# A displaced, smoothed residual on one core: shorter tile heads, narrower frame copies, and another order of the blocks

## The chip, the cores and the metric

The kernel runs on one core of one Trainium2 chip. The metric is the device time of one execution in microseconds (us), as the median of three runs. PE is the matrix engine (TensorE), DVE the vector engine (VectorE), ACT ScalarE, POOL GpSimd; SP (SyncE) only issues DMAs here, and all loads and stores go through its one queue.

## The reference, cut to what matters

`x` is 16 images of 768 channels of 64 x 64 float32 values, `offset` 48 pairs of displacements. The result is `x + conv(shift(group_norm(x)))`:

```python
# group norm: 32 groups of 24 channels, mean and variance over (24, 64, 64) of one image
n = (x - mean) / sqrt(var + 1e-5)
off_px = offset * 64                        # 48 positions, each for 16 neighbouring channels
off_int = round(off_px); sub = off_px - off_int
dx, dy = off_int[:, 0], off_int[:, 1]       # one pair for each position
shifted[r, c] = n[r - dy, c - dx]           # zero where that lies outside the 64 x 64 image
kern = exp(-((kx + sub_x)**2 + (ky + sub_y)**2) / 0.5), normalised   # 3 x 3, kx and ky in -1, 0, 1
out = x + conv3x3(shifted, kern, padding="SAME")                     # each channel by itself
```

The offsets are a 7 x 7 grid without its centre, from -48 to 48 pixels in steps of 16 in both directions, each moved by a random number of deviation 0.64 pixels. A large displacement leaves only a small window of the image that gets anything added.

## The kernel before, in words

**Tiles.** One tile is one position (16 channels) of 8 images: 128 partitions of 4096 float32 values, 2.1 MB. There are 48 positions and two halves of the images, so 96 tiles, and each is loaded once and stored once in place: SBUF holds ten slots of one tile each (`xs`, `SLOTS`). Three neighbouring positions are a block (48 channels, two groups); a block of one half is a unit, so there are 32 units of three tiles.

**Statistics of a unit.** PE sums the tiles of the next unit over the partitions (L289, 16 instructions a tile). ACT reduces that sum (L463), PE spreads it (L304 to L306), ACT copies it out as means (L470, L476), and squares each tile against its mean (L484, about 3.9 us with its accumulator read). PE spreads the squares (`variances`, L346 to L354), ACT scales them (L492), and POOL makes from them three column weights for each tile (L253, then L257, L260, L266 three times).

**The tile itself.** ACT copies the rows of the tile that the window needs into `frame`, with the mean subtracted (`fill_frame`, L417); `frame` has a border of zeros. DVE then makes five passes over the window, all of them SCALAR_TENSOR_TENSOR: L704 and L709 smooth along the row into `smooth`; L713, L716 and L719 add the smoothed rows to the tile in `xs` with the three column weights. Window heights and widths are rounded up to one of four sizes, `SIDES = [64, 50, 34, 18]`, and each of the 16 combinations is a branch of its own, chosen at run time from a word read into a register (`choose`, L185). For this the loop over tiles (`tile_of`, L751) has a head of register instructions: the loop's own, L727, L732, the branches, and L704's addresses. L708 reads the four words of the next tile.

**What waits for what.** `frame` is single: ACT may fill it for the next tile once L709 of this one is done. L713 needs the column weights of its tile. POOL's weights need the variances, which for the heavier unit of a pair need the first two tiles of the next unit loaded and summed, since PE runs its instructions in the written order.

**Order of the units.** `PAIRS` lists pairs of blocks. A pair (a, b) gives four units: a and b of the first half of the images, a and b of the second. The window sizes (rows x columns) of the three tiles of each block, worked out from the offsets:

| Block | Tiles | Block | Tiles |
|---|---|---|---|
| 0 | 18x18, 18x34, 18x50 | 8 | 64x50, 64x34, 64x18 |
| 1 | 18x64, 18x50, 18x34 | 9 | 50x18, 50x34, 50x50 |
| 2 | 18x18, 34x18, 34x34 | 10 | 50x64, 50x50, 50x34 |
| 3 | 34x50, 34x64, 34x50 | 11 | 50x18, 34x18, 34x34 |
| 4 | 34x34, 34x18, 50x18 | 12 | 34x50, 34x64, 34x50 |
| 5 | 50x34, 50x50, 50x64 | 13 | 34x34, 34x18, 18x18 |
| 6 | 50x64, 50x34, 50x18 | 14 | 18x34, 18x50, 18x64 |
| 7 | 64x18, 64x34, 64x50 | 15 | 18x50, 18x34, 18x18 |

**SP's queue.** Ten loads, then in a fixed order stores and loads: the store of tile n waits until DVE has finished that tile (L202), the load of tile n + 10 until the store of tile n has landed (L197). The queue is in order, so a store whose tile is late holds up the loads behind it. The last load is issued after the store of tile 86, and only stores follow.

**Setup.** DVE works out all table entries in `smooth` (L581 to L669), one instruction after another, each waiting for the one before; then it sums the third tile (L677), which the first unit's means need.

Of the kernel before, what the change touches and what calls it, by code (L numbers as in the profile page):

```python
# [5 lines left out]
def build(nc, x, offset, out):  # L6
    f32 = mybir.dt.float32
    i32 = mybir.dt.int32
# [4 lines left out]
    P = 128  # L13
# [10 lines left out]
    UT = 3  # L24
# [21 lines left out]
    PAIRS = [(9, 4), (3, 13), (5, 0), (7, 2), (10, 14), (8, 1), (6, 11), (12, 15)]  # L46
# [13 lines left out]
    KIND, TO, FROM, COLUMN = range(WORDS)  # L60
    ROW_BITS = (H - SIDES[-1]).bit_length()

    ctx = ExitStack()
    with ctx:
# [19 lines left out]
        small = sb("small", [P, 54])  # L84
# [9 lines left out]
        col_flat = small[:, 27:45]  # L94


        own_mean = small[:, 45:48]
        own_sum = small[:, 48:49]
        mean_64 = small[:, 49:51]
        spread = small[:, 51:53]  # L100

        last_sum = small[:, 53:54]
        col_w = col_flat.rearrange("p (u k) -> p u k", k=3)
        base_w = xs[:, SLOTS * PIX:].rearrange("p (n k) -> p n k", k=3)
        side_w = [sb(f"side_w{k}", [P, TILES]) for k in range(2)]
        words = sb("words", [P, WORDS * (TILES + 1)], i32)
        fills = sb("fills", [P, TILES], i32)
# [15 lines left out]
        word_of = words[:, 0:WORDS * TILES].rearrange("p (n k) -> p n k", k=WORDS)  # L123
# [102 lines left out]
        def _(pool):  # L226
# [13 lines left out]
            for i in range(2 * UT):  # L240
                V.memset(word_of[:, :, COLUMN].rearrange("p (u i) -> p u i", i=2 * UT)[:, :, i], 3 * i)

            V.memset(words[:, WORDS * TILES:], 0).then_inc(slots_ready, 1)
# [6 lines left out]
            def weights(u):  # L250
# [4 lines left out]
                for i in range(UT):  # L255
# [10 lines left out]
                    V.tensor_scalar(col_w[:, now * UT + i, :], base_w[:, position, :], rstd0[:, column],  # L266
# [111 lines left out]
        def _(act):  # L378
# [13 lines left out]
            def load_fill(n):  # L392
                act.reg_load(entry, fills[0:1, bass.ds(n, 1)])  # L393

            def fill_frame(u, i, last=False):


                word = act.snap(entry, min_val=0, max_val=(len(SIDES) << ROW_BITS) - 1)
                row = word & (1 << ROW_BITS) - 1
                rows_kind = act.snap(word >> ROW_BITS)  # L400
# [4 lines left out]
                act.reg_mov(copy_from, base + row * W)  # L405
                act.reg_mov(copy_to, row * PITCH + PAD * PITCH)
# [3 lines left out]
                def emit(k):  # L410
                    rows = SIDES[k]
                    a = act.snap(copy_from, min_val=0, max_val=(SLOTS - 1) * PIX + (H - rows) * W)
                    b = act.snap(copy_to, min_val=PAD * PITCH, max_val=(PAD + H - rows) * PITCH)
                    if not first:

                        act.wait_ge(smooth_ready, act.snap(frames, min_val=1, max_val=TILES))
# [360 lines left out]
```

## Time and profile before

| | us |
|---|---|
| median of 3 runs (973.67 to 978.83) | 973.79 |
| the profiled execution's own time | 979.06 |
| its span | 977.1 |
| DVE busy | 824.8 (84%) |
| PE busy | 785.6 (80%) |
| ACT busy | 638.9 (65%) |
| POOL busy | 368.1 (38%) |
| DMA, share of 16 engines | 98.0% |
| bytes moved | 403.09 MB, mean 413 GB/s |

The profile's page divides the span into 40 slices and gives for each the busy tenths of every engine, and the rate of the DMA engines. A line of the list of groups, or of the list by shape, says which line of the kernel ran on which engine, how often, its busy time and its mean duration; behind it stands how long the engine was idle just before, and what it waited for. Windows give the same busy times for stretches of the span. Every duration in this document is of the one profiled execution, whose time is 979.06 us.

### The profile page before, as it was taken

How to read it: one execution, taken by the hardware profiler on the slowest of the kernel's cores; microseconds unless marked ns; L12 is line 12 of the kernel's file. 1: busy time of each engine (PE TensorE's matmuls, PEld its weight loads, DVE VectorE, ACT ScalarE, POOL GpSimd, SP SyncE). 2: the span in 40 equal slices, each digit the busy share in tenths (PEclk: the TensorE clock that was granted, in tenths of full speed). 3: DMA queues.
4: the chain of work that ended last, by engine and by line, in shares of the span. 5: the costliest groups of instructions: out<-in, count | busy, mean ns of one | idle time of the engine just before them, and what ended most of it. 6: DMA issues, size and time to landing. Idle time of an engine off the chain costs nothing.

```text
span 977.1 us, 9088 instructions
## 1 busy us (share of the span) xinstructions
PE 785.6 (80%) x2132; PEld 383.6 (39%) x2132; DVE 824.8 (84%) x551; ACT 638.9 (65%) x461; POOL 368.1 (38%) x348
## 2 busy tenths in 40 slices
PE   0998987979979698897979879689797997979820
PEld 0544443434434343353434434345343443434410
DVE  7587988777798997978889899898998979797795
ACT  7778676564766747678466746577675785774661
POOL 0214034340432624013254393463845438250312
PEclk9999988989979799897998979989898897989955
DMA  9999999999999999999999999999999999999948
GB/s 364 427 401 423 392 405 429 429 429 428 430 429 430 432 428 414 430 429 430 431 429 406 398 433 376 407 419 393 431 408 430 430 427 431 431 431 430 430 208 343
DMA packets 27821, 403.09 MB, mean 413 GB/s; under 512 B 3216, under 2 KB 3216, under 8 KB 3216
## 3 DMA queue, kind: packets, MB, share of 16 engines
q1 hardware_dynamic: 27792, 402.71, 98.0%
q8 instruction: 17, 0.28, 0.1%
q14 instruction: 12, 0.10, 0.0%
HBM read 201.38 MB, written 201.33 MB: 412 GB/s over the span
## 4 chain that ended last, share of the span: by engine, by line
DVE 28%; DMA 27%; PE 20%; POOL 7%; issue 7%; ACT 5%; DVEq 3%; ACTq 2%; SPq 0%; POOLq 0%
PE sum_ps L289 17%; DMA out_dram<-xs 15%; DMA xs<-x_dram 12%; DVE xs L713 6%; DVE xs L716 6%; DVE smooth L709 6%; DVE smooth L704 6%; DVE xs L719 4%; POOL small L253 2%; POOL small L260 2%; ACT frame L417 2%; POOL small L257 2%; ACT unused L484 2%; POOL small L266 1%; ACTq L393 1%
## 5 line engine op out<-in xcount | busy, mean ns | idle before, releaser
L289 PE MATMUL sum_ps<-xs,bands 128*128 128x512 f32 x976 | 483.5, 653 | 51.2 <-DMA xs<-x_dram 51.2
L484 ACT ACTIVATE unused<-xs,small 128x4096 bf16 (+1 forms) x94 | 348.3, 3706 | 8.3 <-ACT small L470 4.8
L417 ACT ACTIVATE frame<-xs,small (+1 forms) x96 | 223.3, 2326 | 184.3 <-DVE smooth L709 183.3
L289 PEld LDWEIGHTS sum_ps<-xs,bands 128*128 128x128 f32 x976 | 200.6, 210 | 295.4 <-issue 282.2
L253 POOL TENSOR_TENSOR small<-small 128x3 f32<-128x3 f32 x32 | 41.6, 1299 | 570.6 <-ACT small L492 570.6
L289 PE MATMUL sum_ps<-xs,halves 128*128 128x512 f32 x496 | 230.0, 619 | 17.4 <-DMA xs<-x_dram 17.4
L704 DVE SCALAR_TENSOR_TENSOR smooth<-frame,side_w 128x612 f32 (+5 forms) x96 | 163.6, 1705 | 72.2 <-ACT frame L417 37.1
L713 DVE SCALAR_TENSOR_TENSOR xs<-smooth,small,xs 128x612 f32 (+5 forms) x96 | 163.5, 1703 | 51.9 <-POOL small L266 49.6
L709 DVE SCALAR_TENSOR_TENSOR smooth<-frame,side_w,smooth x96 | 159.7, 1664 | 7.5 <-DVE smooth L704 4.1
L719 DVE SCALAR_TENSOR_TENSOR xs<-smooth,small,xs 128x594 f32 (+9 forms) x96 | 159.8, 1664 | 3.4
L716 DVE SCALAR_TENSOR_TENSOR xs<-smooth,small,xs 128x594 f32 (+9 forms) x96 | 159.7, 1664 | 3.4
L289 PEld LDWEIGHTS sum_ps<-xs,halves 128*128 128x128 f32 x496 | 97.4, 199 | 146.4 <-issue 119.3
L266 POOL TENSOR_SCALAR small<-xs,small 128x3 f32<-128x3 f32 x96 | 119.5, 1245 | 9.5
L260 POOL TENSOR_SCALAR small<-small 128x1 f32<-128x1 f32 x96 | 106.6, 1110 | 8.4
L257 POOL TENSOR_SCALAR small<-small 128x1 f32<-128x1 f32 x96 | 99.7, 1039 | 3.3
L463 ACT ACTIVATE sum_ps<-sum_ps 128x512 f32<-128x512 f32 x31 | 18.0, 581 | 73.8 <-PE sum_ps L289 71.0
L304 PE MATMUL mean_ps<-small,halves 128*128 128x1 f32 x62 | 13.0, 279 | 61.6 <-ACT sum_ps L463 61.6
L304 PEld LDWEIGHTS mean_ps<-small,halves 128*128 128x128 f32 x62 | 10.7, 217 | 74.3 <-ACT sum_ps L463 74.3
L470 ACT ACTIVATE small<-mean_ps 128x3 f32<-128x3 f32 x31 | 5.4, 175 | 27.6 <-PE mean_ps L306 27.6
L492 ACT ACTIVATE small<-var_ps,small 128x3 f32<-128x3 f32 x32 | 8.2, 255 | 22.6 <-PE var_ps L354 21.7
L346 PEld LDWEIGHTS var_ps<-small,bands 128*128 128x128 f32 x62 | 11.9, 194 | 18.8 <-issue 18.8
L484 ACT ACTIVATION_READ_ACCUMULATOR unused<-xs,small 128x1 f32 x94 | 17.5, 186 | 0.0
(132 smaller groups left out, 259.3 us busy)
## 6 DMA issues: line engine op xcount, KB each, us to landing
xs<-x_dram SPq DMA_DIRECT2D x96, 2048.0 KB, 14.8
out_dram<-xs SPq DMA_DIRECT2D x96, 2048.0 KB, 17.7
smooth<-offset_dram SPq DMA_DIRECT2D x1, 48.0 KB, 4.1
```

The lines of the kernel that those rows point to most:

```text
L253: V.tensor_tensor(rstd0, var, power, ALU.pow).then_inc(rstd_step, 1)
L257: V.tensor_scalar(fix[:, column], var[:, column], rstd0[:, column], rstd0[:, column], ALU.mult, ALU.mult).then_inc(rstd_step, 1)
L260: V.tensor_scalar(rstd[:, column], fix[:, column], -0.5, 1.5, ALU.mult, ALU.add).then_inc(rstd_step, 1)
L266: V.tensor_scalar(col_w[:, now * UT + i, :], base_w[:, position, :], rstd0[:, column], rstd[:, column], ALU.mult, ALU.mult).then_inc(col_w ...
L289: last = nc.tensor.matmul(sum_ps[:, :], (FIRST, SAME, SECOND)[i], slot_px(n, c * BANK, (c + 1) * BANK), start=(i == 0 and c == 0), stop=(i ...
L417: nc.scalar.activation(frame[:, bass.ds(b, rows * PITCH)].rearrange("p (r c) -> p r c", c=PITCH)[:, :, LEFT:LEFT + W], xs[:, bass.ds(a, ro ...
L484: nc.scalar.activation(unused[:, :], xs[:, bass.ds(n % SLOTS * PIX, PIX)], ACT.Square, bias=neg_mean[:, i:i + 1], accum_out=squares[:, i:i ...
L704: V.scalar_tensor_tensor(sm, frame_window(beside, cols), side_w[0][:, bass.ds(n, 1)], frame_window(src, cols), ALU.mult, ALU.add).wait_op( ...
L709: V.scalar_tensor_tensor(part, frame_window(behind, cols - 1), side_w[1][:, bass.ds(n, 1)], part, ALU.mult, ALU.add).wait_op(half_smooth, ...
L713: V.scalar_tensor_tensor(x_window(0, rows), sm, col_flat[:, bass.ds(weights + 1, 1)], x_window(0, rows), ALU.mult, ALU.add).wait_op(smooth ...
L716: V.scalar_tensor_tensor(x_window(1, rows), sm[:, 0:rows - 1], col_flat[:, bass.ds(weights, 1)], x_window(1, rows), ALU.mult, ALU.add).wai ...
L719: V.scalar_tensor_tensor(x_window(0, rows - 1), sm[:, 1:rows], col_flat[:, bass.ds(weights + 2, 1)], x_window(0, rows - 1), ALU.mult, ALU. ...
```

## The change

It has three parts.

**Heads and words.** The tile loop now counts from 1, so that the loop's register is itself the count that semaphores are compared with. The register instructions of L727 and L732 (copies of the count, the address to the side, the address behind) are gone from the head: the address to the side is now a word of its own (`BESIDE`, in place of `COLUMN`), and the address behind is worked out between the first and the second pass. The column of weights is found by a remainder, `done % (2 * UT)`, in the address of each of the three adding passes. The read of the next tile's words moves from between the first and second pass to between the second and third. The column weights have a buffer of their own with another layout, and the words for ACT lie in the other 64 partitions of `words`.

In the DVE program, the head of the tile loop and the first two passes of one branch (18 x 18) before; `words` is the table of words, `side_w` the weights along the row, ISA a register instruction:

```order
L751 ISA
L727 REGISTER_ALU
L727 ISA
L732 ISA
L185 COMPARE_AND_BRANCH x4
L704 ISA
L704 SCALAR_TENSOR_TENSOR smooth<-frame,side_w 128x324
L708 ISA
L708 TENSOR_LOAD words
L709 ISA
L709 SCALAR_TENSOR_TENSOR smooth<-frame,side_w,smooth 128x18x17
```

And the same place now, up to the third pass:

```order
L773 ISA
L191 COMPARE_AND_BRANCH x4
L730 ISA
L730 SCALAR_TENSOR_TENSOR smooth<-frame,side_w 128x324
L737 ISA x2
L737 SCALAR_TENSOR_TENSOR smooth<-frame,side_w,smooth 128x18x17
L741 ISA
L741 TENSOR_LOAD words
L743 ISA
L743 SCALAR_TENSOR_TENSOR xs<-smooth,col_w,xs 128x18x18
```

Three register instructions have left the head, one has come between the first two passes, and the read of the words has moved behind the second.

**Narrow copies.** Where the window is 34 or 18 columns wide, ACT copies only 34 columns into `frame`: 64 x 34 for windows of 64 or 50 rows, 34 x 34 for those of 34 or 18. The word for ACT now holds a column too. Setup works out these words with more instructions. In the DVE program's setup, from the first row number to the words of ACT (`fills`), before:

```order
L635 TENSOR_TENSOR smooth<-smooth 128x96
L637 SCALAR_TENSOR_TENSOR smooth<-smooth 128x48
L639 CAST fills<-smooth 128x96
L640 ISA
L642 SCALAR_TENSOR_TENSOR smooth<-smooth 128x48
```

And now:

```order
L643 TENSOR_TENSOR smooth<-smooth 128x96
L648 TENSOR_SCALAR smooth<-smooth 128x48
L649 TENSOR_SCALAR smooth<-smooth 128x48
L650 TENSOR_TENSOR smooth<-smooth 128x48
L651 TENSOR_TENSOR smooth<-smooth 128x48
L652 TENSOR_TENSOR smooth<-smooth 128x48
L654 TENSOR_SCALAR smooth<-smooth 128x48
L655 TENSOR_SCALAR smooth<-smooth 128x48
L656 TENSOR_TENSOR smooth<-smooth 128x48
L657 SCALAR_TENSOR_TENSOR smooth<-smooth 128x48
L658 SCALAR_TENSOR_TENSOR smooth<-smooth 128x48
L659 TENSOR_TENSOR smooth<-smooth 128x48
```

Behind these follow L660, L661 and the cast of L663; two more (L678, L679) make the new word. That is 14 instructions more in the chain that ends with the sum of the third tile.

**Order.** Another `PAIRS`. SP's, PE's and POOL's programs keep their order of instructions but for the six memsets of `COLUMN` on POOL; they move other tiles. The core of the diff:

```diff
-    PAIRS = [(9, 4), (3, 13), (5, 0), (7, 2), (10, 14), (8, 1), (6, 11), (12, 15)]
+    PAIRS = [(12, 1), (10, 15), (8, 14), (7, 13), (6, 11), (5, 2), (3, 4), (9, 0)]
...
-    KIND, TO, FROM, COLUMN = range(WORDS)
+    KIND, TO, FROM, BESIDE = range(WORDS)
+    NARROW = 2
+    COPIES = [(rows, W) for rows in SIDES] + [(SIDES[k], SIDES[NARROW]) for k in (0, NARROW)]
...
-            for i in range(2 * UT):
-                V.memset(word_of[:, :, COLUMN].rearrange("p (u i) -> p u i", i=2 * UT)[:, :, i], 3 * i)
...
-                    V.tensor_scalar(col_w[:, now * UT + i, :], base_w[:, position, :], rstd0[:, column],
+                    V.tensor_scalar(col_w[:, :, (now * UT + i + 1) % (2 * UT)], base_w[:, position, :], rstd0[:, column],
                                     rstd[:, column], ALU.mult, ALU.mult).then_inc(col_w_ready, 1)
...
             def fill_frame(u, i, last=False):
-                word = act.snap(entry, min_val=0, max_val=(len(SIDES) << ROW_BITS) - 1)
-                row = word & (1 << ROW_BITS) - 1
-                rows_kind = act.snap(word >> ROW_BITS)
+                word = act.snap(entry, min_val=0, max_val=(len(COPIES) << ROW_BITS + COL_BITS) - 1)
+                column = word & (1 << COL_BITS) - 1
+                row = (word >> COL_BITS) & (1 << ROW_BITS) - 1
+                copy_kind = act.snap(word >> ROW_BITS + COL_BITS)
...
-                act.reg_mov(copy_from, base + row * W)
-                act.reg_mov(copy_to, row * PITCH + PAD * PITCH)
+                act.reg_mov(copy_from, base + row * W + column)
+                act.reg_mov(copy_to, row * PITCH + column + PAD * PITCH)
...
                     nc.scalar.activation(
-                        frame[:, bass.ds(b, rows * PITCH)].rearrange("p (r c) -> p r c", c=PITCH)[:, :, LEFT:LEFT + W],
-                        xs[:, bass.ds(a, rows * W)].rearrange("p (r c) -> p r c", c=W),
+                        frame[:, bass.ds(b, rows * PITCH)].rearrange("p (r c) -> p r c", c=PITCH)[:, :, LEFT:LEFT + cols],
+                        xs[:, bass.ds(a, rows * W)].rearrange("p (r c) -> p r c", c=W)[:, :, 0:cols],
                         ACT.Identity, bias=fill_mean[:, i:i + 1]).then_inc(frame_ready, 1)
...
                 dve.wait_ge(frame_ready, done)
-                V.scalar_tensor_tensor(sm, frame_window(beside, cols), side_w[0][:, bass.ds(n, 1)], frame_window(src, cols),
+                V.scalar_tensor_tensor(sm, frame_window(beside, cols), side_w[0][:, bass.ds(done, 1)], frame_window(src, cols),
                                        ALU.mult, ALU.add
                                        ).wait_op(tile_done, done_count, "sem-ge").then_inc(half_smooth, 1)
-                dve.reg_load(next_tile, words[0:1, bass.ds(done * WORDS, WORDS)])
-                V.scalar_tensor_tensor(part, frame_window(behind, cols - 1), side_w[1][:, bass.ds(n, 1)], part,
+                turn = kind_of % 2
+                behind = (src + 1 - turn).with_bounds(min_val=1, max_val=most + 1)
+                V.scalar_tensor_tensor(part, frame_window(behind, cols - 1), side_w[1][:, bass.ds(done, 1)], part,
                                        ALU.mult, ALU.add
                                        ).wait_op(half_smooth, done_count, "sem-ge").then_inc(smooth_ready, 1)
+                dve.reg_load(next_tile, words[0:1, bass.ds(done * WORDS, WORDS)])
                 dve.wait_ge(col_w_ready, done)
-                V.scalar_tensor_tensor(x_window(0, rows), sm, col_flat[:, bass.ds(weights + 1, 1)], x_window(0, rows),
+                V.scalar_tensor_tensor(x_window(0, rows), sm, col_w[:, 0, bass.ds(done % (2 * UT), 1)], x_window(0, rows),
                                        ALU.mult, ALU.add
                                        ).wait_op(smooth_ready, done_count, "sem-ge").then_inc(centre_added, 1)
...
-            def tile_of(n):
-                dve.reg_mov(done_count, n + 1)
-                done = dve.snap(done_count, min_val=1, max_val=TILES)
+            def tile_of(done):
+                dve.reg_mov(done_count, done)
                 kind_of = dve.snap(next_tile[KIND], min_val=0, max_val=2 * len(SIDES) ** 2 - 1)
-                dve.reg_mov(at_turn, kind_of & 1)
-                turn = dve.snap(at_turn, min_val=0, max_val=1)
...
-                dve.reg_mov(at_behind, src + 1 - turn)
-                dve.reg_mov(at_beside, src + 2 * turn - 1)
...
-            with dve.Fori(0, TILES) as n:
+            with dve.Fori(1, TILES + 1) as n:
                 tile_of(n)
```

## Rows read from the trace of the kernel before

**Rows 1.** The page: DMA rate in 40 slices of 24.4 us; the bytes.

```profile
GB/s 364 427 401 423 392 405 429 429 429 428 430 429 430 432 428 414 430 429 430 431 429 406 398 433 376 407 419 393 431 408 430 430 427 431 431 431 430 430 208 343
DMA packets 27821, 403.09 MB, mean 413 GB/s; under 512 B 3216, under 2 KB 3216, under 8 KB 3216
```

**Rows 2.** Windows: us, busy of each engine, PEclk, DMA share, GB/s.

```profile
60.00:140.00 80.00, 70.57 (x197) 34.04 (x196) 69.04 (x47) 61.84 (x45) 22.86 (x30) 0.94 0.99 400
...
530.00:740.00 210.00, 175.49 (x472) 85.63 (x471) 191.41 (x107) 135.26 (x99) 109.09 (x70) 0.89 0.99 407
...
930.00:977.00 47.00, 4.88 (x20) 4.56 (x20) 34.64 (x25) 18.30 (x15) 9.72 (x13) 0.51 0.65 275
```

**Rows 3.** Windows of DVE alone: us, DVE busy, PEclk, DMA share, GB/s.

```profile
260.70:382.60 121.90, 107.85 (x60) 0.88 1.01 426
...
501.00:627.30 126.30, 116.35 (x61) 0.91 0.98 405
627.30:746.70 119.40, 107.36 (x61) 0.89 1.00 416
```

**Rows 4.** DVE's waits over the whole span: us in total, times, longest.

```profile
DVE smooth L704 <- DVE xs L719: 19.1, 30, 1.0
DVE smooth L704 <- issue: 14.8, 13, 1.5
```

**Rows 5.** By shape: DVE's first pass, largest and smallest window.

```profile
L704 DVE SCALAR_TENSOR_TENSOR smooth<-frame,side_w 128x3200 f32 x10 | 35.6, 3557 | 6.9 <-DVE xs L719 3.7 <-ACT frame L417 3.0
...
L704 DVE SCALAR_TENSOR_TENSOR smooth<-frame,side_w 128x324 f32 x8 | 4.4, 556 | 4.3 <-issue 4.1
```

**Rows 6.** The chain that ended last, a tile's head: start us, us, what.

```profile
958.49 0.06 DVE xs L719
...
959.42 0.22 DVEq L727
...
959.68 0.17 DVEq L732
...
960.48 0.09 DVE smooth L704
...
960.61 0.93 DVEq L708
```

**Rows 7.** Line L425, a remainder in registers: ns minimum/median/maximum.

```profile
L425 ACTq FUSED_REGOPS  x95: 120/133/163, 27.8 to 956.1; - x95
```

**Rows 8.** Timeline of the start, DVE: start us, us, what, [idle before].

```profile
13.36 0.21 DVE L637 SCALAR_TENSOR_TENSOR smooth<-smooth 128x48 f32<-128x48 f32 x1
13.61 0.21 DVE L639 CAST fills<-smooth 128x96 int32<-128x96 f32 x1
...
20.33 4.42 DVE L677 TENSOR_REDUCE small<-xs 128x1 f32<-128x4096 f32 x1 [1.11 <-DMA xs<-x_dram]
...
37.83 1.16 DVE L713 SCALAR_TENSOR_TENSOR xs<-smooth,small,xs 128x900 f32 x1 [5.06 <-POOL small L266]
```

**Rows 9.** Timeline of SP's queue: start us, until its last issue, DMA.

```profile
41.36 11.36 SPq L202 DMA_DIRECT2D out_dram<-xs  x2
60.93 5.17 SPq L197 DMA_DIRECT2D xs<-x_dram  x2
...
906.85 63.22 SPq L202 DMA_DIRECT2D out_dram<-xs  x9
```

**Rows 10.** Timeline of the end, DVE and ACT.

```profile
923.92 1.99 DVE L713 SCALAR_TENSOR_TENSOR xs<-smooth,small,xs 128x1700 f32 x1 [2.10 <-POOL small L266]
...
935.27 2.13 ACT L417 ACTIVATE frame<-xs,small  x1 [10.88 <-DVE smooth L709]
...
951.27 1.25 ACT L417 ACTIVATE frame<-xs,small  x1
...
956.16 1.15 DVE L713 SCALAR_TENSOR_TENSOR xs<-smooth,small,xs 128x900 f32 x1 [1.11 <-POOL small L266]
```

**Rows 11.** Timeline of POOL beside a heavy tile (64 columns, 50 rows).

```profile
500.97 3.67 POOL L257 TENSOR_SCALAR small<-small 128x1 f32<-128x1 f32 x1
```

More of the change, by code:

```diff
@@ L83, in build @@
         halves = sb("halves", [P, 2, BIND, IMAGES])
-        small = sb("small", [P, 54])
+        small = sb("small", [P, 36])
+        col_w = sb("col_w", [P, 3, 2 * UT])
         zeros = small[:, 0:1]
@@ L93, in build @@
         rstd0, fix, rstd = (small[:, 18 + i * UT:18 + (i + 1) * UT] for i in range(3))
[L94 to L103, printed above, removed]
+        own_mean = small[:, 27:30]
+        own_sum = small[:, 30:31]
+        mean_64 = small[:, 31:33]
+        spread = small[:, 33:35]
+        last_sum = small[:, 35:36]
         base_w = xs[:, SLOTS * PIX:].rearrange("p (n k) -> p n k", k=3)
-        side_w = [sb(f"side_w{k}", [P, TILES]) for k in range(2)]
+        side_w = [sb(f"side_w{k}", [P, TILES + 1]) for k in range(2)]
         words = sb("words", [P, WORDS * (TILES + 1)], i32)
-        fills = sb("fills", [P, TILES], i32)
+        fills = words[HALF:P, 0:TILES]
         setup = smooth[:, 0:11 * 2 * POSITIONS].rearrange("p (n f a) -> p n f a", n=11, a=2)
@@ L667, in _ @@
             chained(V.tensor_tensor(tmp[:, :, 0], tmp[:, :, 0], norm[:, :, 1], ALU.mult))
-            for k in range(3):
-                last = V.tensor_tensor(base_w[:, :, k], e[:, k, :, 1], tmp[:, :, 0], ALU.mult)
+            for i, k in enumerate((1, 0, 2)):
+                last = V.tensor_tensor(base_w[:, :, i], e[:, k, :, 1], tmp[:, :, 0], ALU.mult)
             steps[0] += 1
@@ L680, in _, with smooth_tile @@
             V.engine_nop().then_inc(tile_done, 1)
-            next_tile = [dve.alloc_register(name) for name in ("next_kind", "next_to", "next_from", "next_column")]
+            next_tile = [dve.alloc_register(name) for name in
+                         ("next_kind", "next_to", "next_from", "next_beside")]
             done_count = dve.alloc_register("done_count")
-            at_turn, at_beside, at_behind = (dve.alloc_register(name) for name in ("turn", "beside", "behind"))
-            def smooth_tile(rows, cols, src, beside, behind, turn, dst, n, done, weights):
+            def smooth_tile(rows, cols, src, beside, kind_of, most, dst, done):
                 under = xs[:, bass.ds(dst, rows * W)]
@@ L741, in emit @@
                     smooth_tile(rows, cols, src.with_bounds(min_val=1, max_val=most),
-                                beside.with_bounds(min_val=0, max_val=most + 1),
-                                behind.with_bounds(min_val=1, max_val=most + 1), turn,
+                                beside.with_bounds(min_val=0, max_val=most + 1), kind_of, most,
                                 dst.with_bounds(min_val=0, max_val=(SLOTS - 1) * PIX + (H - rows) * W + W - cols),
-                                n, done, weights)
+                                done)
                 choose(dve, kind_of, 0, len(SIDES) ** 2, emit, 2)
```

65 lines of the change are left out of this document (42 added, 23 removed).

## The prediction

> **What bounds the kernel now.** I read the page's slices first, then windows over the stretches in which they differ, then DVE's waits there, and last the two ends in the timeline.
>
> The reader should see that the DMA engines set most of the time. In slices that nothing disturbs they move 428 to 432 GB/s [rows 1]; at 430, the 403.09 MB take 937.4 us of the span of 977.1. The other 39.7 us are the places where the rate falls, and each can be priced as its length times its shortfall over 430. From 60 to 140 us it is 400, which loses 80 x 30/430 = 5.6 us. From 530 to 740 it is 407: 210 x 23/430 = 11.2 us. From 930 to the end it is 275: 47 x 155/430 = 16.9 us [rows 2]. The first 60 us lose about 4 (the first slice has 364), and the rest is spread in parts of a GB/s.
>
> Why does it fall in the middle? SP stores a tile only when DVE has finished it, and a late store holds the loads behind it. Six tiles (a pair of blocks, one half of the images) are 12 transfers of 2.097 MB, 25.2 MB, so DMA needs 58.5 us for them. DVE took 126.3 us for twelve tiles from 501.0, the pair (10, 14), which is 63.2 for six, with 58.2 of it busy [rows 3]. There DVE is the bound: DMA would have been through in 117. The next twelve took 119.4 and the rate still was 416; the lag was being worked off. The pair (5, 0), from 260.7, took 121.9 with 107.9 busy, and the rate was 426 [rows 3]: the slots absorb a lag of some 5 us, not of 15.
>
> At the end DVE and the statistics are the bound. SP has nothing left but nine stores from 906.85 on, each waiting for its tile [rows 9].
>
> **The order.** The five passes of a tile take, by the largest and smallest window, 0.218 us each and 1.043 ns an element (3557 ns for 3200, 556 for 324) [rows 5]. The second pass has a column less, the last two a row less. For the blocks this gives, in us: 0 and 15, 12.7; 1 and 14, 16.9; 2 and 13, 14.0; 3 and 12, 32.0; 4 and 11, 17.0; 5 and 10, 41.4; 6, 33.2; 7 and 8, 36.9; 9, 29.6. So six tiles cost before, pair by pair, 46.6, 46.0, 54.1, 50.9, 58.3, 53.8, 50.2, 44.7, and now 48.9, 54.1, 53.8, 50.9, 50.2, 55.4, 49.0, 42.3. The sum stays; the largest goes from 58.3 to 55.4.
>
> To this comes what DVE idles between tiles. In six tiles of (10, 14) it was (126.3 - 116.35)/2 = 5.0 us, in six of (5, 0) (121.9 - 107.85)/2 = 7.0, a part of it waiting for DMA's side [rows 3].
>
> **The heads.** After the start of L719 DVE's sequencer goes through the head: 958.49 to 960.48, 2.0 us [rows 6]. Where L719 is shorter than that, the rest is idle. L727 and L732 took 0.22 and 0.17 us there, with the plain copy and the gaps between some 0.5. All of it goes, so after each tile with under about 1,700 elements 0.5 us of idle goes. L704's waits for L719 and for "issue", which are these heads, sum to 33.9 us in 43 places [rows 4], 0.8 each. Six tiles of the heavy pairs have three or four light tiles, so they save 1.5 to 2.0 us. The read of the words, 0.93 us [rows 6], only changes the pass that covers it: between the first two it is now uncovered by 0 and after the second by as much as before. I take 0; the ends are -0.3 and +0.3 us a tile for windows of 18 x 18 and 18 x 34, which is nothing for most of the run, since DMA covers it. The remainder in the three adding passes costs what the one on ACT does, 0.13 us [rows 7], and runs under a pass of at least 0.55: 0.
>
> So six tiles of (10, 15) need about 54.1 + 4.1 = 58.2 us, (8, 14) 57, (5, 2) 55.4 + 4.2 = 59.6, the others under 56. Against DMA's 58.5, only (5, 2) lags, by 2 us over its twelve tiles, and the pair (5, 0) showed that 5 cost nearly nothing. I let 1.2 of the 11.2 us stand: **-10.0 us**. The bounds are -11.2 (no dip left) and -5 (the heavy pairs follow each other now, and each leaves half a dip).
>
> **Narrow copies.** A copy took 2.13 us at 34 rows and 1.25 at 18, both 64 wide [rows 10], so 0.88 us per 1,024 elements, and by that 3.0 at 50 rows and 3.8 at 64. 64 x 34 are 2,176 elements, the 2.13; 34 x 34 are 1,156, the 1.25. It saves 0.85 us on most tiles of the blocks 2, 4, 6, 9, 11, 13 and 1.6 on four positions of 7 and 8. ACT's 65% hide all of it but in light units, where DVE waits for the frame; there DMA now covers it. I take 0 outside the start and the end, at most -1.
>
> **The start.** Fourteen instructions of setup come in, at 0.25 us from one start to the next [rows 8]: 3.5 us. DVE had 1.11 us to spare before L677, so that sum ends 2.4 us later. PE, the variances and POOL follow it in a chain, so L713 of the first tile goes from 37.8 to 40.2 [rows 8]. The first tile is 34x50 now, not 50x18: its three adding passes end at 46.1 in place of 41.3. The second (34x64, 12.3 us) ends at 58.5 in place of 52.4. SP's order is store, store, load, load [rows 9]; the ten loads and the first store are 23.1 MB, moved by about 57.5 us. Before, the second store reached the queue 5 us ahead of that, and now 1 us behind it, with its latency on top. The third tile ends at 68.4 (67.8 before), the sixth at about 87.6 (88.1), so the loss stays near the front: **+2.0 us**, between -2 (the dips to 140 us shrink with lighter heads) and +4.
>
> **The end.** In the last heavy unit the weights of its first tile set the clock: L713 at 923.92 [rows 10], after the load of the tile before the last two. I count from there. Before, ACT's copy for the third tile came at 11.4, behind the second pass of a 34x64; then 2.1 of copy and 18.8 of statistics led to L713 of the last unit at 32.2, and the last tile ended at 45.8 (SP's last issue, of 0.34 us, was through at 970.07 [rows 9]). Now the unit is 9: its first tile's adding passes take 3.5 us, 0.4 of head, and two passes of 50x34 3.9, so the copy starts at 7.9. It is 50 rows at full width, 3.0, which gives 10.9 + 18.8 = 29.7. DVE itself gets through 50x34 and 50x50 (9.8 and 14.0) at 27.7 and through the first two passes at 29.0: it waits 0.7. Then 1.7 of adding passes, 0.9 of head, 4.2 + 0.3, 0.6, and 5.7: 43.4. That is **-2.4 us**. The last store follows after the last tile as before (7.4 us to the span's end). The bounds are 0 and -4.
>
> In this stretch one rule of the notes speaks against me. POOL's L257, with one column of work, took 3.67 us beside a first pass of 3.56 [rows 5, 11]: POOL's small operations wait for a pass of DVE to end. The Trainium skill has this in "SBUF — State Buffer", section "SBUF: two separate sides": the pair of ports that the two share is an exclusive lock, and the loser is blocked for the whole instruction. The trace agrees. Here the passes beside the last weights are 2.8 us long, not 2.0, so by it each of POOL's first two could end up to 0.8 later: the gain of the end would be 0.8 instead of 2.4. In my times DVE is through with the long passes 1.3 us after the variances come, so only one of POOL's four meets one, and I keep 2.4.
>
> **Sum.** -10.0 + 2.0 - 2.4 = -10.4 us. Against the profiled execution (span 977.1, time 979.06) this is 966.7 and 968.7. The median, 973.79, is 5.3 below that execution; I take the same difference from it: **963.4 us**.
>
> **The rivals.**
> - *The middle is cleaner than I allow.* All dips go and the start costs nothing, since the first dips (5.6 us) shrink with the lighter heads: -11.2 - 2 - 2.4 = -15.6, 958. For it: only one pair is above 58.5. Against: the start has later stores.
> - *Half the gain.* The three heaviest pairs but one stand second to fourth, when DVE has just caught up, and each drops the rate as (8, 1) did behind (10, 14). The middle gives -5, the end -1, the start +2: 969.8. For it: the rate was still 416 with 53.8 us of busy [rows 3]. Against: that was the lag of the pair ahead.
> - *The dips are DMA's own.* Then no order helps, and start and end cancel (+2.0 - 2.4): 973.4. Against: they lie exactly where DVE is busy 191 of 210 us [rows 2].
> - *Slower: the remainder sits on DVE's path.* ACT's took 0.13 us under other work [rows 7]; if on DVE three of them and the moved read of the words each leave 0.25 us uncovered, six tiles gain 6 us of idle and lose 2: 9.0 in place of 5.0. With that the pairs stand at 57.9, 63.1, 62.8, 59.9, 59.2, 64.4, 58.0 and 51.3; twice what is above 58.5 is 33.8 us of loss for the present 11.2. The slots absorb some 5, so +17.6, with start and end 991. It decides from about 7 us of idle in six tiles on, 1.2 a tile, against 0.8 now in (10, 14). Against: the shortest pass is longer than four such remainders.
>
> **How the numbers follow.** About 0.5% (4.9 us) is what a measurement of this kernel can tell from no change. Chances: the forecast 0.62 (959.5 to 967.5), cleaner 0.14, half the gain 0.12 (968 to 972), DMA's own 0.07, slower 0.05. Faster than 968.9 are the first two and half of the third, 0.82; within are the other half and the fourth, 0.13; slower 0.05. The range 957 to 971 leaves out the last two and an edge of the second and third.
>
> **What would show it.** The rate in every slice from the sixth to the 37th is 425 or more; if the second to fourth pairs (the slices 6 to 20) have dips, my account of the lag is wrong. DVE's waits for L704 by "issue" and L719 fall from 33.9 us over the run to under 15. L704 follows L719's start by 1.5 us in light tiles. DVE's first adding pass starts at 40.2, and the second store at about 58.5. From the first weights of the last heavy unit to the end of the last tile it is 43.4 us. The forecast is wrong if twelve tiles of (10, 15) take over 120 us without DVE waiting for POOL at their start.

## The result and the profile after

| | before | changed |
|---|---|---|
| median of 14 runs, us | 977.11 (973.67 to 978.88) | 970.03 (967.83 to 974.41) |
| profiled execution, us | 979.06 | 969.93 |
| its span, us | 977.1 | 967.8 |

The ratio to the kernel before is 0.994, with a 95% interval of 0.9927 to 0.9952: some 5 to 7 us faster. 963.4 was forecast, 10.4 us under a median of three runs, and the changed kernel is 6.6 us above that.

The page's rates, answering to [rows 1]:

```profile
GB/s 363 429 372 414 429 422 431 428 430 429 428 427 429 431 429 428 431 432 431 431 429 425 429 427 426 413 416 406 430 423 416 429 429 430 432 431 431 429 219 347
```

And the windows that answer to [rows 2]; the columns are as there:

```profile
60.00:140.00 80.00, 74.85 (x211) 36.20 (x210) 72.80 (x48) 55.70 (x45) 35.42 (x30) 0.96 1.01 418
140.00:500.00 360.00, 307.17 (x837) 148.53 (x837) 322.49 (x185) 223.91 (x170) 163.66 (x121) 0.91 1.01 429
530.00:740.00 210.00, 181.47 (x499) 87.66 (x498) 182.22 (x108) 128.12 (x99) 82.24 (x72) 0.90 1.00 420
740.00:920.00 180.00, 152.50 (x414) 73.12 (x413) 141.48 (x94) 110.09 (x85) 59.80 (x67) 0.91 1.01 430
920.00:967.80 47.80, 5.71 (x22) 4.57 (x21) 36.36 (x26) 19.18 (x15) 8.36 (x13) 0.55 0.67 282
```

The dip around 540 us is gone, and the slices 26 to 31 hold one that wasn't forecast: 413, 416, 406, 430, 423, 416. The forecast wanted 425 or more from the sixth slice to the 37th; the sixth has 422, and the 7th to the 25th have 425 or more. It lies on the sixth pair, (5, 2), whose twelve tiles ran from 615.5 to 736.1. DVE's window there, answering to [rows 3]:

```profile
615.50:736.10 120.60, 110.61 (x60) 0.89 1.00 415
```

That is 60.3 us for six tiles, 59.6 being forecast. The pair (10, 15), second in the order, took 119.8 us from its first pass to that of the next pair, for a forecast of 116.4 and a bound of 120; its rate was 429. DVE's waits, answering to [rows 4]:

```profile
DVE xs L743 <- POOL col_w L270: 66.3, 31, 7.4
DVE smooth L730 <- ACT frame L425: 27.4, 19, 5.1
DVE smooth L730 <- DVE xs L749: 13.9, 31, 0.9
DVE xs L743 <- DVE smooth L737: 5.1, 14, 0.8
```

L730's wait for heads is 13.9 us where it was 33.9, under the 15 that were forecast. The read of the words, now before the third pass, leaves 5.1 us of waiting there, where it left 4.1 before the second. In the chain that ended last, a head between two light tiles, answering to [rows 6]:

```profile
953.44 0.06 DVE xs L749
...
954.90 1.17 DVE smooth L730
...
956.19 0.96 DVEq L741
...
957.20 0.14 DVEq L743
```

From L749 to L730 it is 1.5 us, not 2.0. The remainder takes 0.14, and here it isn't hidden: it comes behind the read of the words, and the third pass starts 0.16 us after the end of the second.

The start and SP's queue, answering to [rows 8, 9]:

```profile
22.95 4.42 DVE L704 TENSOR_REDUCE small<-xs 128x1 f32<-128x4096 f32 x1
...
40.89 1.99 DVE L743 SCALAR_TENSOR_TENSOR xs<-smooth,col_w,xs 128x1700 f32 x1 [4.28 <-POOL col_w L270]
```

```profile
46.86 12.84 SPq L208 DMA_DIRECT2D out_dram<-xs  x2
...
899.07 62.11 SPq L208 DMA_DIRECT2D out_dram<-xs  x9
```

The sum of the third tile starts 2.6 us later, the first adding pass 3.1, the second store at 59.4. The end, answering to [rows 10], first DVE, then ACT:

```profile
916.50 1.16 DVE L743 SCALAR_TENSOR_TENSOR xs<-smooth,col_w,xs 128x900 f32 x1 [3.21 <-POOL col_w L270]
...
946.88 0.56 DVE L743 SCALAR_TENSOR_TENSOR xs<-smooth,col_w,xs 128x324 f32 x1 [1.16 <-POOL col_w L270]
...
959.72 1.10 DVE L749 SCALAR_TENSOR_TENSOR xs<-smooth,col_w,xs 128x850 f32 x1
```

```profile
924.56 2.99 ACT L425 ACTIVATE frame<-xs,small  x1 [7.00 <-DVE smooth L737]
```

Counted from 916.50, ACT's copy comes at 8.1 (7.9 forecast), the last unit's first adding pass at 30.4 (29.7), the end of the last tile at 44.3 (43.4).

**The losses by stretch.** The text ahead priced a stretch as its length times its shortfall from 430 GB/s, over 430. With the same rule for one profiled execution of every kernel, in us; the last column but one is the last 50 us of the span. In the last column stands the median of the timed runs.

| Kernel | 0-140 | 140-500 | 500-740 | 740 to the end | last 50 | median, us |
|---|---|---|---|---|---|---|
| before | 9.4 | 0.8 | 11.2 | 0.0 | 17.6 | 976 to 977 |
| changed | 8.5 | 0.8 | 5.0 | 0.0 | 16.4 | 970.03 |
| order_only | 6.8 | 5.0 | 8.9 | 0.0 | 17.7 | 973.73 |
| no_order | 9.1 | 0.0 | 5.6 | 0.0 | 17.7 | 971.51 |
| wide_copies | 11.1 | 0.0 | 4.5 | 0.4 | 18.4 | 970.64 |
| own_sum_early | 7.2 | 0.8 | 3.9 | 2.1 | 17.7 | 969.61 |
| swap_5_10 | 9.1 | 0.8 | 3.9 | 0.0 | 16.5 | 969.69 |
| best | 7.8 | 0.0 | 0.0 | 2.9 | 18.4 | 969.59 |
| five_two_second | 8.8 | 1.7 | 2.8 | 0.0 | 15.3 | 970.19 |
| five_with_0 | 8.8 | 0.8 | 2.8 | 0.4 | 18.0 | 971.18 |
| drain_57 | 11.1 | 0.0 | 9.5 | 0.0 | 14.1 | 972.24 |
| one_load_a_store | 10.7 | 0.0 | 1.7 | 0.0 | 15.2 | 966.59 |
| old_order_one_load | 8.8 | 0.0 | 3.9 | 0.0 | 16.9 | 970.84 |
| one_load_early_sum | 7.2 | 0.0 | 3.3 | 0.0 | 14.8 | 965.88 |
| combined | 11.7 | 1.7 | 0.6 | 8.2 | 15.2 | 968.69 |
| four_passes | 7.2 | 0.0 | 0.0 | 4.8 | 11.2 | 965.11 |
| four_passes_drain | 9.1 | 0.0 | 8.4 | 0.0 | 9.0 | 966.31 |

So the profiled execution won 9.3 us of span: 6.2 in the middle, 1.2 at the end, 0.9 at the start, and 1.0 that the rounded rates don't place. How far one row can be trusted shows in two kernels that have the changed kernel's order and nearly its program: `wide_copies` and `own_sum_early` lost 4.5 and 3.9 in the middle, for its 5.0. The start is worse: from 60 to 140 us kernels with the new order had anything from 390 to 418 GB/s, those with the old one 400 to 404, so the 0.9 of the start is within what executions differ by.

### The profile page after: what moved, and what is told of

The parts are those of the page before. It is cut to its first block, busy times and chain, and to the rows that moved or that the text cites. A ratio compares the mean times of both kernels' runs of the same rounds, so it can differ in the third digit from the quotient of the medians.

```text
span 967.8 us, 9186 instructions
## 1 busy us (share of the span) xinstructions
PE 778.9 (80%) x2132; PEld 379.0 (39%) x2132; DVE 827.6 (86%) x565; ACT 599.7 (62%) x461; POOL 382.6 (40%) x342
## 4 chain that ended last, share of the span: by engine, by line
DMA 43%; PE 26%; DVE 18%; POOL 5%; issue 3%; ACT 2%; DVEq 1%; ACTq 1%; SPq 0%; POOLq 0%
DMA out_dram<-xs 27%; PE sum_ps L293 23%; DMA xs<-x_dram 16%; DVE xs L743 4%; DVE xs L746 4%; DVE xs L749 3%; DVE smooth L730 2%; DVE smooth L737 2%; POOL small L261 2%; POOL small L264 1%; POOL small L257 1%; ACT unused L492 1%; ACT frame L425 1%; POOL col_w L270 0%; DVE small L704 0%
## 5 line engine op out<-in xcount | busy, mean ns | idle before, releaser
L425 ACT ACTIVATE frame<-xs,small (+1 forms) x96 | 183.4, 1910 | 179.6 <-DVE smooth L737 176.0
L257 POOL TENSOR_TENSOR small<-small 128x3 f32<-128x3 f32 x32 | 40.2, 1255 | 545.1 <-ACT small L500 545.1
L743 DVE SCALAR_TENSOR_TENSOR xs<-smooth,col_w,xs 128x1700 f32 (+5 forms) x96 | 163.5, 1704 | 73.2 <-POOL col_w L270 66.3
L730 DVE SCALAR_TENSOR_TENSOR smooth<-frame,side_w 128x1700 f32 (+5 forms) x96 | 163.6, 1704 | 43.3 <-ACT frame L425 27.4
L746 DVE SCALAR_TENSOR_TENSOR xs<-smooth,col_w,xs 128x1650 f32 (+9 forms) x96 | 159.8, 1664 | 3.4
L749 DVE SCALAR_TENSOR_TENSOR xs<-smooth,col_w,xs 128x1650 f32 (+9 forms) x96 | 159.8, 1664 | 3.4
L270 POOL TENSOR_SCALAR col_w<-xs,small 128x3 f32<-128x3 f32 x96 | 123.7, 1288 | 9.5
L264 POOL TENSOR_SCALAR small<-small 128x1 f32<-128x1 f32 x96 | 113.4, 1181 | 8.4
L261 POOL TENSOR_SCALAR small<-small 128x1 f32<-128x1 f32 x96 | 104.8, 1092 | 3.3
L350 PEld LDWEIGHTS var_ps<-small,bands 128*128 128x128 f32 x62 | 11.9, 194 | 18.8 <-issue 18.8
## 6 DMA issues: line engine op xcount, KB each, us to landing
xs<-x_dram SPq DMA_DIRECT2D x96, 2048.0 KB, 14.8
```

Source lines behind the costliest of these rows:

```text
L257: V.tensor_tensor(rstd0, var, power, ALU.pow).then_inc(rstd_step, 1)
L261: V.tensor_scalar(fix[:, column], var[:, column], rstd0[:, column], rstd0[:, column], ALU.mult, ALU.mult).then_inc(rstd_step, 1)
L264: V.tensor_scalar(rstd[:, column], fix[:, column], -0.5, 1.5, ALU.mult, ALU.add).then_inc(rstd_step, 1)
L270: V.tensor_scalar(col_w[:, :, (now * UT + i + 1) % (2 * UT)], base_w[:, position, :], rstd0[:, column], rstd[:, column], ALU.mult, ALU.mul ...
L425: nc.scalar.activation(frame[:, bass.ds(b, rows * PITCH)].rearrange("p (r c) -> p r c", c=PITCH)[:, :, LEFT:LEFT + cols], xs[:, bass.ds(a, ...
L730: V.scalar_tensor_tensor(sm, frame_window(beside, cols), side_w[0][:, bass.ds(done, 1)], frame_window(src, cols), ALU.mult, ALU.add).wait_ ...
```

## The experiments

Ratios are to the kernel before, run on the same chip, with 95% intervals. Unless said otherwise the edit is made to the changed kernel.

**The parts.** `order_only` is the kernel before with the new `PAIRS`; `no_order` the reverse:

```diff
-    PAIRS = [(12, 1), (10, 15), (8, 14), (7, 13), (6, 11), (5, 2), (3, 4), (9, 0)]
+    PAIRS = [(9, 4), (3, 13), (5, 0), (7, 2), (10, 14), (8, 1), (6, 11), (12, 15)]
```

> The kernel before with the new PAIRS alone (old heads, wide copies, short setup). Theory 'late stores': what counts is how much DVE needs for six tiles against DMA's 58.5 us, and idle heads count in it. Without the shorter heads six tiles of (10, 15) need about 60, of (5, 2) about 61.5, so the dips stay in part: ratio to the kernel before 0.996 (0.994 to 0.999). Rival 'the order is all of it': 0.993 to 0.994, as the whole change. Rival 'the heads are all of it': 1.000.

> The changed kernel with the old PAIRS: heads, words and narrow copies without the order. Theory 'late stores': six tiles of (10, 14) fall from 63.2 to about 61.5 us, still over 58.5, so some 3 to 4 us of the middle go, the start loses up to 2 by the longer setup: ratio 0.997 (0.995 to 1.000). Rival 'the order is all of it': 1.000 to 1.003. Rival 'the heads are all of it': 0.993.

Measured: 0.9972 (0.9956 to 0.9988) and 0.9957 (0.9940 to 0.9974). Each is near its forecast by lateness of stores, and neither rival holds: the gain is two parts, some 3 and 4 us, that add up to the whole within their intervals. The profiled execution of `order_only` (978.21 us) lies 4.5 above its median, so its row in the table probably overstates its dips.

`wide_copies` puts no tile into the narrow class:

```diff
-            chained(V.tensor_scalar(narrow, kind[:, :, 0], float(NARROW), None, ALU.is_ge))
+            chained(V.tensor_scalar(narrow, kind[:, :, 0], 99.0, None, ALU.is_ge))
```

> The changed kernel with every copy of ACT 64 columns wide, setup chain as long as in the changed kernel. Theory 'late stores': ACT is hidden by DMA except where DVE is the bound in light units; the ratio to the kernel before is as the changed kernel's, 0.994, or up to 0.996. Rival 'the copies carry a third of the gain or more': 0.996 to 0.998, with L730 waiting for ACT's frame over 40 us in place of 27.4.

0.9937 (0.9919 to 0.9954): the narrow copies are worth nothing that can be measured, to within some 2 us, though L730 waits 36.3 us for ACT in place of 27.4.

`own_sum_early` moves the sum of the third tile:

```diff
+            dve.wait_ge(loaded[UT - 1], 16)
+            V.tensor_reduce(own_sum, slot_px(UT - 1), ...)
+            ...
             dve.wait_ge(exps_ready, 1)
             chained(V.tensor_tensor(norm[:, :, :], e[:, 0], e[:, 1], ALU.add))
```

> The changed kernel with the sum of the third tile (L704) moved ahead of the last 11 setup instructions, so that the longer setup no longer delays it. Theory 'the setup delays the first store': the first adding pass goes from 40.9 to about 38.6 us, the second store from 59.3 to 57, and the whole by up to 2.3 us: ratio 0.992. Rival 'the later dips swallow it': first pass earlier, time as the changed kernel's, 0.994.

DVE's timeline there:

```profile
21.24 4.42 DVE L686 TENSOR_REDUCE small<-xs 128x1 f32<-128x4096 f32 x1 [0.56 <-DMA xs<-x_dram]
...
39.69 1.99 DVE L743 SCALAR_TENSOR_TENSOR xs<-smooth,col_w,xs 128x1700 f32 x1 [4.27 <-POOL col_w L270]
```

0.9923 (0.9902 to 0.9945), 969.61 us. The first adding pass came 1.2 us earlier, not 2.3: the sum now waits for its tile, whose last part landed at 21.15 us in that execution, where it was 20.29 in the changed kernel's. The interval holds both the forecast and the changed kernel's 0.994: inconclusive.

**Does the sum of six tiles decide?** Three other orders. `five_with_0` has (5, 0) as sixth pair and (9, 2) last; `swap_5_10` exchanges blocks 5 and 10; `best` is written out in its expectation.

> The changed kernel with the blocks 2 and 0 exchanged: pair six is (5, 0), 54.1 us of passes in place of 55.4, and the last pair (9, 2). Theory 'the sum of six tiles decides': the loss from 600 to 740 us falls from 4.3 to under 2 us, the end takes about 1.3 us longer (14.0 in place of 12.7): ratio 0.992 to 0.993. Rival 'the heaviest tile last decides': loss stays at 4, the end costs 1.3: 0.995.

> The changed kernel with the blocks 5 and 10 exchanged: pair two is (5, 15), pair six (10, 2); all sums of six tiles stay. Block 5 has its heaviest tile last, block 10 first. Theory 'the sum of six tiles decides': the dip stays at the sixth pair (600 to 740 us, about 4 us lost), time as the changed kernel's, 0.994. Rival 'the heaviest tile last decides': the dip moves to the second pair (140 to 260 us) and 600 to 740 us lose under 1.5.

> The early sum, and another order: (12, 1), (10, 15), (3, 4), (5, 0), (8, 2), (7, 14), (6, 11), (9, 13). No pair above 54.1 us, the two heaviest with a pair of 49 between them. Theory 'the sum of six tiles decides': no slice from 140 us to the last 50 loses over 1 us, start as with the early sum; ratio 0.988 to 0.991. Rival 'the dips come anyway where a heavy unit begins': 0.992 or more.

Measured: 0.9952 (0.9937 to 0.9968), 0.9927 (0.9911 to 0.9944), 0.9939 (0.9917 to 0.9962). With (5, 0) at 54.1 us instead of 55.4, 500 to 740 us still lost 2.8 us, where under 2 was forecast, and the last 50 us lost 1.6 more than in the changed kernel (1.3 forecast). In `swap_5_10` the loss stayed at the sixth pair (3.9 us there, 0.8 from 140 to 500), so it isn't block 5's tile order; but the early (5, 15) lost nothing. `best` has no loss up to 740 us and then one of 2.9, beside pairs of only 50.2 and 43.6 us. So `five_with_0` and `best` are misses for my first theory. `swap_5_10` came out as it said, but with a sum of 54.1 us that cost nothing early and, in `five_with_0`, 2.8 us late. The time in the run counts, and not the sum alone.

**A pass less.** `four_passes` is without L746, so it doesn't compute the whole result:

> The changed kernel without the pass L746, so the row above is left out of the result; DVE has one fifth less to do, DMA the same bytes. Theory 'late stores': the dips after the start are DVE's, so from 140 us to the last 50 the rate is 428 or more in every slice (under 1.5 us lost in place of 6.6), the last 50 us lose some 5 us less, together a ratio to the kernel before of 0.980 to 0.986. Rival 'the dips are DMA's own': the slices at 600 to 740 us stay at 405 to 425 and only the end gets shorter, 0.988 to 0.990.

0.9892 (0.9862 to 0.9922). The dips from 500 to 740 us vanish, as DVE's should, but the ratio misses the 0.980 to 0.986 of that theory, since a new dip comes after 740, with DVE idle four tenths of the time; the columns are DVE busy, PEclk, DMA share, GB/s:

```profile
740.00:911.00 171.00, 104.81 (x70) 0.90 1.01 418
```

So there are two kinds of dips, and the end of this run has one that a lighter DVE didn't cure. In the trace each transfer has 16 completion signals, as many as the core has DMA engines, and I take each to stand for one engine's part. I took the time from the first to the last of the 16 for every transfer, and averaged over stretches that begin at the times shown (us):

```
                     140  260  380  500  620  740  860-910
before               3.1  4.1  5.1  4.4  2.4  4.5  5.7
changed              3.9  5.0  6.2  7.2  6.3  5.3  6.5
best                 2.8  3.4  4.2  4.9  6.6  7.0  7.7
four_passes          2.8  3.2  4.2  5.6  6.9  7.3  7.5
four_passes_drain    3.4  3.2  3.7  5.2  2.3  3.7  3.8
drain_57             3.2  4.1  5.5  6.9  2.4  3.9  3.9
combined             3.3  4.2  4.5  6.0  6.7  7.3  8.0
```

While the stream is full the parts drift apart, and where it starves they come level again. A load may go only when all 16 parts of a store have landed, so the drift takes from the slots' slack: a few us late in the run.

The same signals show where that slack ends. For each transfer I took the margin: how long after the end of its issue the first part of the transfer issued ahead of it landed. Over all runs, from 140 to 900 us, first parts follow each other by 4.9 us on average where the margin is 3 us or more, and by 5.8 where it is between 0 and 1. Three loads of `four_passes`, and the loads at the same place of `four_passes_drain` (us; the last two columns are the time since the first and the last part of the transfer ahead):

```
                     load issued   margin   first part   last part
four_passes              836.2       1.8        5.9         5.2
four_passes              856.9       1.6        5.9         4.9
four_passes              877.4       1.8        5.9         4.9
four_passes_drain        840.9       5.6        4.9         4.9
four_passes_drain        860.4       5.6        4.9         4.9
```

Each of the three loads comes 1 us too late for the first part, while the last part follows nearly at its pace. From 740 us on the least margin of a load was 1.6 to 1.7 us in the four kernels that lose 2 us or more there (`four_passes`, `own_sum_early`, `best`, `combined`), and 2.2 to 5.5 in the thirteen others, which lose 0.4 at most.

**Testing the drift.** `five_two_second` exchanges the pairs (5, 2) and (10, 15). `drain_57` adds this to SP's list:

```diff
             for n in range(TILES):
+                if n == 57:
+                    for s in range(SLOTS):
+                        sp.wait_ge(loaded[s], 16 * len(range(s, next_load, SLOTS)))
+                        sp.wait_ge(stored[s], 16 * len(range(s, n, SLOTS)))
                 store(n)
```

> The changed kernel with the pairs (5, 2) and (10, 15) exchanged: (5, 2), 55.4 us of passes, is the second, (10, 15), 54.1, the sixth. Theory 'the DMA engines drift apart': the 16 completion signals of a transfer lie 3 to 4 us apart early and 7 later, and that uses up the slots' slack, so a heavy pair late loses and early it doesn't: under 1.5 us lost at 140 to 260 us, 3 to 4 at 620 to 740, time as the changed kernel's. Rival 'the sum of six tiles decides': the loss moves with (5, 2): 4 us at 140 to 260, under 1.5 at 620 to 740.

> The changed kernel, but SP waits once, ahead of the store of tile 57 (about 590 us), until every transfer issued so far has landed. Theory 'the DMA engines drift apart': the drain costs 4 to 8 us where it stands and puts the 16 engines level (spread back to 3 to 4 us), so the sixth pair behind it, 640 to 760 us, loses under 2 us in place of 4.3. Rival 'the sum of six tiles decides': the sixth pair loses 4 or more, since the drain leaves DVE's demand as it is and takes transfers away.

> four_passes (without the pass L746, whose row above is missing from the result) with the one wait for all transfers ahead of the store of tile 57. Theory 'the DMA engines drift apart': four_passes lost 4.9 us from 740 to 911 us while DVE was idle half the time; with the engines put level at about 590 us that stretch loses under 1.5 us and their spread stays under 5, while the drain itself costs 5 to 8. Rival 'something late in the run slows DMA': 740 to 911 us lose 4 or more as before.

`five_two_second`, second and sixth pair:

```profile
135.00:256.00 121.00, 106.22 (x282) 50.45 (x282) 108.80 (x62) 75.27 (x57) 45.39 (x40) 0.89 1.01 430
620.00:740.00 120.00, 103.90 (x277) 49.78 (x276) 108.55 (x62) 75.05 (x57) 67.91 (x44) 0.90 1.00 419
```

The heavier pair in the early place loses nothing in this window, and 0.6 us in its own, from 141.1 to 263.3 (428 GB/s). The lighter in the late place loses 120 x 11/430 = 3.1 us, though its twelve tiles took 118.2 us and the heavier pair's 122.2: as the drift has it. The ratio is 0.9928 (0.9911 to 0.9946). `drain_57`, first the changed kernel over its sixth pair, then `drain_57` (PEclk, DMA share, GB/s):

```profile
615.00:740.00 125.00, 107.33 (x298) 52.18 (x297) 114.69 (x63) 74.21 (x57) 46.63 (x42) 0.89 1.00 415
```

```profile
590.00:640.00 50.00, 0.84 0.86 349
640.00:765.00 125.00, 0.88 1.01 428
```

The drain costs 50 x 81/430 = 9.4 us where it stands (4 to 8 forecast), and the same pair behind it loses 0.6 in place of 4.4. The whole is 0.9946 (0.9931 to 0.9960). One rival this run leaves: while SP waited 14.4 us for the transfers, DVE went on with loaded tiles, so it had a start on the stores of the next pair. That was a part of it, since from 640 to 765 us SP waited 18.8 us for DVE, for 27.7 in the changed kernel. But the spread shows beside it. In the changed kernel a store of this pair, issued at 658.5, came 7.6 us ahead of the last part of the transfer before it and only 0.6 ahead of the first, and the first part was 1.2 us late. Behind the drain one issued at 723.2 had 8.2 and 4.6, and none was late. And `four_passes_drain`, DVE's windows as above:

```profile
740.00:911.00 171.00, 108.53 (x71) 0.92 1.01 430
```

430 instead of 418, with the drain 100 us earlier and nothing else changed, and DVE idle over a third of the time: with the margins above, the late dip is the drift's. The drain's own stretch, 500 to 740 us, lost 8.4 us (5 to 8 forecast). The ratio, 0.9906 (0.9884 to 0.9928), shows that the drain doesn't pay.

**SP's list.** In the light units two stores stood ahead of two loads:

```diff
-            AGAIN = [(-1,), (0,), (1,), (), (2, 3), (4,)]
+            AGAIN = [(-1,), (0,), (1,), (2,), (3,), (4,)]
```

> The changed kernel with one load behind each store in SP's list, where two stores and then two loads stood in the light units. Theory 'finished stores stand behind waiting loads': in the light unit a store now waits for one landing at most, so the dips at 620 to 740 us shrink by half (4.3 to about 2) and the ratio is 0.991 to 0.993. Rival 'what is in flight decides, not its order': as the changed kernel, 0.994, or slower by up to 2 us, since the third store's load now stands ahead of the fifth store.

0.9889 (0.9871 to 0.9906), 966.59 us in the median, the four runs within 1.1 us: the largest single step in ratio, and beyond both forecasts. SP's queue there, one load and one store about every 10 us:

```profile
611.31 0.34 SPq L203 DMA_DIRECT2D xs<-x_dram  x1
611.69 0.70 SPq L208 DMA_DIRECT2D out_dram<-xs  x1
621.12 0.34 SPq L203 DMA_DIRECT2D xs<-x_dram  x1
621.50 0.67 SPq L208 DMA_DIRECT2D out_dram<-xs  x1
```

From 500 to 740 us it loses 1.7 us, not 5.0. The least margin of a load there is 3.0 us, where it was 1.7.

> The changed kernel's heads and copies with the old PAIRS, and one load behind each store. Theory 'order and list are two things': (10, 14) still needs about 61.5 us of DVE for six tiles, so 3 us or more are lost at 500 to 740 us, and the kernel is 2 to 4 us slower than the new order with the same list: ratio 0.992 to 0.994. Rival 'the order gained only by what stood behind waiting loads': with the list mended, the old order is as good as the new one, 0.989.

> The changed kernel with the early sum, one load behind each store, and the heavy pairs ahead of the light ones: (12, 1), (10, 15), (5, 2), (8, 14), (7, 13), (6, 11), (3, 4), (9, 0). Theory 'the engines drift apart and eat the slack': heavy pairs early, while the engines are level, lose under 1 us together, the sixth pair now is a light one (50.2 us), and nothing is lost from 140 us to the last 50: ratio 0.984 to 0.988. Rival 'the list of SP was all of it': as with one load behind each store alone, 0.989.

> The changed kernel with one load behind each store and the early sum. If the start's gain stays: up to 2 us under one_load_a_store, ratio 0.986 to 0.988. If the drift takes it back later: 0.989.

The old order with this list had 0.9941 (0.9921 to 0.9962), so order and list are two things, and the order is worth some 4 to 5 us with this list. The list alone is less sure than its best run: on the changed kernel the ratio fell by 0.005, on `own_sum_early` and on `no_order` by 0.002, which is within their intervals, and `one_load_early_sum` lost 3.3 us from 500 to 740, not 1.7. `combined` missed: 0.9904 (0.9880 to 0.9928) for 0.984 to 0.988, with runs from 963.9 to 976.65. The profiled one is the slowest, 8.0 above the median. It lost this after 740 us, with pairs of 49 us and less:

```profile
740.00:925.00 185.00, 140.96 (x93) 0.92 1.00 411
```

Its spread is 7.3 to 8.0 us there, the largest of the table. `one_load_early_sum` had 0.9905 (0.9884 to 0.9926), for 0.986 to 0.988 or 0.989 forecast, and a median of 965.88 us, the lowest of all kernels that compute the whole result; from `one_load_a_store` it can't be told. Both beat the changed kernel and the one before.

## Why the prediction was wrong

Right: that the DMA rate is the bound and that DVE's lateness has a part in the dips of the middle (`four_passes`); the durations of tiles and heads (60.3 us against 59.6, heads 1.5 us, waits for heads 13.9); copies at nothing; the remainder at nearly nothing; the later first and second stores (40.9 and 59.4 against 40.2 and 58.5); the end's steps to within 0.9 us, for a gain of 1.5 us in place of 2.4.

Wrong, in the order of their size:

- **The middle.** The step was "I let 1.2 of the 11.2 us stand: -10.0 us", and under it "the slots absorb a lag of some 5 us", read from (5, 0) at 260 us. At 620 us they don't: (5, 2), with 120.6 us for twelve tiles where (5, 0) had 121.9, lost 4.4 us. The term measured -6.2 us. A slack read at one time of the run was used at another; the spread of a transfer's 16 parts is 4.1 us there and 6 to 7 here. `five_two_second` shows that the place makes the difference, and the margins and the two drains that it does so through the drift. Both kinds of lateness are in the dip: loads issued at 621.7 and 641.9 with margins of 1.7 and 2.0 us, and stores that waited for DVE at 658.5 and 718.8, with 0.6. A smaller fault lies ahead of it: the 4.1 and 4.2 us of idle in six tiles don't follow from the 5.0 less 1.5 to 2.0 that stand before them, and (5, 2) had 5.0. A part of the loss may also be SP's list, since with one load behind each store the same stretch lost 1.7 to 3.3.
- **The base.** I took the profiled execution's gain from 973.79, the median of three runs of which two were the lowest of 14. The 14 have 977.11, and the profiled execution was 2.0 above that; 10.4 off 977.11 would have been 966.7, and the measured 970.03 is 3.3 above it. So half of the miss of 6.6 us is the base.
- **The start.** It was to lose 2.0 and won 0.9 up to 140 us: the dips behind it shrank (418 GB/s for 400 [rows 2]) while the first 60 us lost more, 6.1 for 4.0. Its bounds held it. The lighter heads, which the prediction gave for such a case, don't show as the reason: `no_order`, with them, had 402 there, and `order_only`, without, 416.
- **The end.** 1.2 to 1.5 for 2.4: the waits between the last three light tiles, 0.9, 0.5 and 0.6 us, were a little longer than taken. The wait of POOL for DVE's passes that was weighed against it wasn't needed: ACT's copy and POOL's weights came within 0.7 us of the forecast.

That the profiled execution's 9.3 us lie so near the 10.4 is luck: the middle fell short by 3.8 and the end by 1.2, while the start came out better by 2.9 and 1.0 isn't placed. Of the rivals, "half the gain" came nearest (969.8), and that is luck too, for its mechanism isn't what happened: not the heavy pairs at places two to four lost, which had 0.8 us together, but the sixth.

What stays open: each stretch is read from one profiled execution, and the timed runs of one kernel lie 1 to 10 us apart (12.7 in `combined`). Why the 16 parts drift apart no run here shows, nor which engine is which among them. So why the list of one load a store helps is argued, not shown: it spreads the waits, and finished stores stand behind one landing at most. What its trace shows is a smaller spread ahead of the heavy pair, 4.0 us for 6.2 from 380 to 500 us, and wider margins.

## What to carry to other kernels

Where a stream of loads and stores is the bound, price the dips of its rate stretch by stretch, and don't carry a slack from one place of the run to another: ask what has happened to it since. Look at the order of issues as well as at the order of the work; moving one load ahead of one store gained 2 to 5 us here, and a new order of all blocks some 2 to 3 with the old list. And take the base from as many runs as the effect needs: two low runs of three made half of the miss.

## What the runs showed of the hardware that wasn't expected

The 16 parts of one 2.1 MB transfer land some 3 us apart from 140 to 260 us of the run, and 6 to 8 us apart after 600 us where the stream hadn't starved since 140 us (`best`, `four_passes`). A gap of some us sets this back: behind the drain of `drain_57` the first transfer's parts landed 0.1 us apart, some 80 us later 3.6, and at 900 us still 3.9. In the four kernels whose loads' least margin fell to 1.7 us or less after 740 us it cost 2 to 8 us there, in `four_passes` with DVE idle four tenths of the time; the others lost 0.4 at most. In these kernels a stream that starves a little in the middle and one that doesn't can so end at the same time: the changed kernel's profiled execution took 969.93 us, that of `best` 968.53.
